# Products of zeros on TensorE in the first attention and the convolution of a four-layer kernel

## The reference

```python
x = x + L0_xattn(layernorm(x), ctx)     # first attention, convolution, MLP
x = x + L0_ffn(layernorm(x))            # 8 experts, 2 a token
x = x + L1_xattn(layernorm(x), ctx)     # second attention
x = x + L1_ffn(layernorm(x))            # 8 gated experts with low-rank parts
```

```python
scores = einsum(Q, K) / sqrt(32)                   # 4 heads, 64 x 64 a sequence
probs  = softmax(top 32 of 64 scores), scattered back
c      = mean over heads of probs @ (ctx @ Wv)
x      = layernorm(x) * (1 + g*scale_in) + g*shift_in   # scale, shift from c @ W_film
y      = causal convolution of x with K, per channel    # K from a sum of 64 exponentials
y      = y * (1 + g*scale_out) + g*shift_out            # from c @ W_film too
```

## Time and profile before

| | us |
|---|---|
| three executions | 932.19, 935.39, 935.05 |
| median | 935.05 |
| span of the profiled execution | 935.4 |
| mean granted clock in it | 0.799 |
| PE busy | 710.3 |
| DVE busy | 673.2 |
| POOL busy | 564.8 |
| ACT busy | 473.4 |

### The profile page before, as it was taken

One profiled execution on the slowest core, in us unless ns is written; L12 is line 12 of the kernel. 1 busy time (PEld: TensorE's weight loads), 2 busy tenths in 40 slices (PEclk: granted clock), 3 DMA queues, 4 the chain that ended last, 5 costly groups with the idle time before them and its releaser, 6 DMA issues. The chain is left out here.

```text
span 935.4 us, 20537 instructions
## 1 busy us (share of the span) xinstructions
PE 710.3 (76%) x6072; PEld 508.4 (54%) x6072; DVE 673.2 (72%) x3212; ACT 473.4 (51%) x1318; POOL 564.8 (60%) x931
## 2 busy tenths in 40 slices
PE   0686898979883999972498528998888874799970
PEld 0353554545483656631275426766666652699970
DVE  6898989978524688769111167598998887699974
ACT  3566576735200455450133175577777761577740
POOL 7688877766526544210677667345777767277770
PEclk9767787957555999996599855798988885899995
DMA  6300112997213977700365330000000002698928
GB/s 143 57 25 10 41 45 64 86 88 96 40 45 140 290 250 257 243 23 0 39 115 132 88 137 1 2 4 13 25 26 25 25 28 76 216 279 264 260 69 270
DMA packets 98829, 94.41 MB, mean 101 GB/s; under 512 B 37511, under 2 KB 82302, under 8 KB 98142
## 3 DMA queue, kind: packets, MB, share of 16 engines
q1 hardware_dynamic: 91268, 79.34, 33.1%
q0 software_dynamic: 6592, 13.58, 6.0%
q10 hardware_dynamic: 858, 0.17, 0.1%
HBM read 47.76 MB, written 43.19 MB: 97 GB/s over the span
## 5 line engine op out<-in xcount | busy, mean ns | idle before, releaser
L2402 POOL DMA_INDIRECT expert_pairs<-e_ys,e_home x78 | 75.4, 967 | 38.4 <-issue 23.5
L1742 POOL TENSOR_SCALAR a_kb<-a_kr,a_m,a_bk 128x128 f32<-128x128 f32 x128 | 57.9, 452 | 44.4 <-ACT a_kr L1981 32.3
L1760 POOL DMA_INDIRECT expert_slots<-r_rows,r_slotu x64 | 63.3, 989 | 30.3 <-DVE r_rows L2136 15.1
L950 DVE MATCH_REPLACE8 work<-m,work 128x64 f32<-128x64 f32 x384 | 75.7, 207 | 0.0
L1484 POOL DMA_INDIRECT ex_rows<-rows,slot_source x32 | 30.7, 960 | 52.7 <-POOLq L1163 43.2
L937 DVE MAX8 m<-work 128x8 f32<-128x64 f32 x384 | 57.0, 209 | 0.0
L825 PE MATMUL psf<-filmw,us 97*128 97x512 f32 x64 | 51.6, 902 | 3.0 <-ACT FO L846 2.9
L1815 PE MATMUL a_pss<-a_kb,a_qt 32*64 32x256 f32 x512 | 41.5, 463 | 13.9 <-ACT a_pp L1966 11.7
L2168 DVE TENSOR_REDUCE a_mx<-a_pss 128x8 f32<-128x512 f32 x64 | 43.9, 686 | 8.1 <-PE a_pss L1815 7.8
L2369 PE MATMUL e_ps<-e_XH,e_wh 128*128 128x256 f32 x156 | 48.1, 308 | 1.5 <-DVE e_XL L2414 1.5
L1536 ACT ACTIVATE ex_hs<-ex_psh,vec 128x512 f32<-128x512 f32 x32 | 22.0, 687 | 51.2 <-PE ex_psh L1517 50.5
(11 more groups left out here) (464 smaller groups left out, 2418.2 us busy)
## 6 DMA issues: line engine op xcount, KB each, us to landing
expert_slots<-rt_unfilled SPq DMA_DIRECT2D x151, 130.0 KB, 2.6
ahead<-folded_weights SPq DMA_DIRECT2D x20, 386.0 KB
e_wf<-folded_weights SPq DMA_DIRECT2D x19, 386.0 KB, 4.2
planes<-rt_zeros SPq DMA_DIRECT2D x4, 1024.0 KB
ew<-in_L_ffn_ew SPq DMA_DIRECT2D x16, 256.0 KB, 4.0
pair_y<-expert_pairs SPq DMA_DIRECT2D x16, 256.0 KB, 5.6
e_xr<-expert_slots SPq DMA_DIRECT2D x27, 130.0 KB, 3.3
folded_weights<-fold_done SPq DMA_DIRECT2D x8, 384.0 KB, 4.3
```

The source lines that it names most:

```text
L950: return own.did(dve.match_replace(wk_[x.j][:, h, :], m8[x.j][:, h, r, :], src[:, h, :], TAKEN))
L1742: m = pool.tensor_scalar(kb[a.j][:, :, h, :], k, m4[:, h:h + 1], bk4[:, h:h + 1], ALU.mult, ALU.add)
L1760: pool.indirect_dma_start(G.slots, bass.IndirectOffsetOnAxis(ap=slot[:, b, k, t:t + 1], axis=0), rb[b % NB][:, k, t, :], None).then_inc(se ...
L2402: pool.indirect_dma_start(G.pair, bass.IndirectOffsetOnAxis(ap=home[i % NY][:, k:k + 1], axis=0), ys[i % NY][:, k, :], None).then_inc(kept ...
```

## The change

A tile `still` of zeros, 128 x 256 in the type F32R (fp32 taken in one pass), is set once by POOL in setup. A helper `fill` issues n products of it, 128 x 128 by 256 columns, into a PSUM region; nobody reads the result. It is called: ahead of the scores (2 products), of the film product (2, and 8 for the last four tiles) and of the turn of `at` (2, and 8 for the last four), each time behind the wait for the bank and ahead of the wait for the data, which are exchanged for this; 12 products at the end of PE's program of the first attention; and 2 behind each of the 8 groups of the convolution, into a bank of their own.

```diff
+def fill(pe, G, out, n):
+    for _ in range(n):
+        pe.matmul(out, G.still[:, 0:P], G.still[:], start=True, stop=True)
...
                 pool.memset(G.dskip[:], 0.0).then_inc(s["memory"], 1)
+                pool.memset(G.still[:].bitcast(F32), 0.0)
                 pool.memset(K.zero, 0.0).then_inc(s["memory"], 1)
...
                     if score.real():
                         j = score.j
+                        after(pe, s["scores_kept"], score.t - 1)
+                        fill(pe, G, pss[j][:, 0:256], 2)
                         pe.wait_ge(s["qk_sb"], score.t + 1)
-                        after(pe, s["scores_kept"], score.t - 1)
...
                     if film.real():
                         j = film.j
+                        after(pe, s["film_sb"], film.t)
+                        fill(pe, G, psf[:, 0:256], 2 if film.t < NT - 4 else 8)
                         pe.wait_ge(s["u_sb"], film.t + 1)
-                        after(pe, s["film_sb"], film.t)
...
                     if attn.real():
+                        after(pe, s["u_sb"], attn.t - 1)
+                        fill(pe, G, psb[attn.j][:, 0:256], 2 if attn.t < NT - 4 else 8)
                         pe.wait_ge(s["attn"], attn.t + 1)
-                        after(pe, s["u_sb"], attn.t - 1)
...
                 march(slot, -3, NT + 3)
+                fill(pe, G, psa[0][:, 0:256], 12)
...
+        unread = C.ps("conv_unread", [P, 256], ctx)[:]
...
                     mm.then_inc(s["y"], 1)
+                    fill(pe, G, unread, 2)
...
+        G.still = C.sb("still", [P, 2 * P], F32R)
```

## The result

| | before | after |
|---|---|---|
| median of 20 runs each, us | 938.28 (929.89 to 944.89) | 932.21 (919.26 to 940.43) |
| ratio after/before | | 0.986, interval 0.983 to 0.989 |
| profiled execution: time, span, us | 935.39, 935.4 | 925.46, 924.2 |
| mean granted clock of the span | 0.80 | 0.85 |
| granted clock from 60 to 240 us | 0.75 | 0.91 |

The account below looks back on a forecast made before the run. DVE was taken to bound the attention at full clock and PE at half, PE the convolution. Attention -7.5, tail -0.5, convolution +1 and memset 0 summed to -7.0 us: 935.05 to 928.0 us, range 912 to 945.

Parts of the forecast that it names:

- Attention, -7.5 forecast: First attention: fills bring the clock back sooner, shortening DVE's stops on `ee`; -7.5 us, from a span of 1.5 to 10.6.
- Nothing below its 6.25 us a tile is to be had: First attention: DVE's busy time, at most 6.25 us for each of 32 tiles, taken as the limit on any gain.
- 3 x 2.8 + 3.3 + 1.7 + 0.3: PE's three attention slots with side pieces at full clock without fills: 13.7 us, against 18.8 us that DVE needs.
- the rival that forecast a loss: Attention slots stay at half clock around "first" and fills only cost; 944 us taken, 954 at worst; chance 0.18.
- "first": Side piece in every third attention slot, four pairs of products, 3.3 or 5.8 us; clock falls inside it were to stay.
- the one near 38: DVE stop of 2.2 us while the attention loop starts up, not PE's; forecast unchanged.
- the one near 195: DVE stop of 3.6 us, where ScalarE waits 5.5 us for a store of folded weights; forecast unchanged.
- The tail, -0.5 forecast: Last four attention tiles: three film products faster at full clock, less their fills; -0.5 us, between -3 and +3.
- the case at half clock: Twelve fills at the attention's end take 2.9 us at half clock, of which 1.1 us would show; 0 was taken.
- The convolution, +1 forecast: Convolution: one or two groups under 2.2 us, then 3.9 us each; +1 us in the sum.
- I let it fall: Convolution with two fills a group: the full clock handed over was taken to fall, after 3.5 us.
- The rival with a chance of 0.12: Clock holds throughout the convolution, all 8 groups at 1.94 us: -11.7 there, -11 in the attention, about 912 us; chance 0.12.

Follow-up runs that it names:

- the corner kernel: The changed kernel with every fill on 32 rows and 32 columns of zeros in place of 128 and 128; ratio 1.070 to the kernel before.
- the kernel with fills only at the end: The changed kernel without fills in the attention's tiles, keeping the 12 at its end and 2 behind each convolution group; ratio 0.993 to the kernel before.
- the pieces: The changed kernel with POOL's 128x1024 product cut into eight, plus 24 fills ahead of each of the first MLP's first two turns; ratio 0.982 to before.

## Why the prediction was right or wrong

**The frame held.** The kernel is faster, by the ratio more than the sum had it. DVE bounds the attention at full clock, PE bounds the convolution, and both depend on the clock. The waits for `ee` were forecast at 13 us and are 12.4 and 12.5 in two profiles, but 24.4 in the third; the clock between 60 and 240 us was forecast at 0.85 and is 0.91, 0.92 and 0.86. The exchanged waits and the memset cost nothing, as forecast, and the kernel with only these shows it.

**Attention, -7.5 forecast, -3.8 measured: mis-sized.** The stops shrank by 8.6 us, which is the mechanism and nearly the size. What was missing is the warning that the prediction itself gave at its end, a stop that moves without touching a term: 3.8 us came back as a longer `pr`, begun while POOL's products ran. "Nothing below its 6.25 us a tile is to be had" held DVE's own work for fixed, and it wasn't. The other profiles add that the gain there is some 3 us in the mean and scatters by more than that.

**The price of the fills: the product right, the change of kind mis-sized.** Behind its like a fill costs 0.12 us at full clock and 0.21 at half, as the row taken for it has it (0.12 and 0.24 forecast). But a fill stands among products of another kind: fp32 products of two records each, or other tile sizes. For that the prediction had 0.1 us a group in the convolution, with a bound of 0.2, and nothing in the attention; in the convolution it is 0.32 at full clock and 0.45 at half, by the groups with no, one and two fills. A pair thus costs 0.56 and 0.87 us a group. In the attention at full clock:
```profile
121.48 0.50 PE L192 MATMUL psb<-still 128*128 128x256 f32 x2
121.82 0.27 PE L849 MATMUL psb<-ident,at 128*128 128x128 f32 x1
121.85 0.48 PE L192 MATMUL pss<-still 128*128 128x256 f32 x2
122.26 0.65 PE L816 MATMUL pss<-kb,qt 128*64 128x256 f32 x4
```
0.34 and 0.41 us a pair, 0.24 of it the two products. Six a tile are thus 1.0 to 1.2 us and not 0.7, with three changes of kind a slot. It did no harm, since DVE bounds there at full clock (3 x 2.8 + 3.3 + 1.7 + 0.3 with 3 x 1.2 makes 17.3, still under 18.8); at half clock it would have made the rival that forecast a loss worse, and the corner kernel is that rival carried out: +7%.

**Which stops go.** Those around "first" behave as the prediction had it: between 90 and 130 us the waits go from 2.6 to 0.5 us (0.7 of the 2.4 near 118 had been forecast to stay). Of the two that were to stay, the one near 38 does, with 2.0 us in place of 2.2; the one near 195, behind the store of folded weights, shrinks from 3.6 to 2.2. Between 50 and 90 us nothing goes (4.4 us, before 4.3), and one stop there has grown from 2.3 to 3.2. The clock of 0.91 is more than the 0.85 that was to be left by the falls inside the side pieces; how many of these went wasn't counted.

**The tail, -0.5 forecast, -0.7 measured,** and the twelve at nothing: right, and for the reason given, since they end at 254.3, before POOL's last product ends at 254.7. The 1.1 us for the case at half clock came out as 0.5 in the kernel with fills only at the end (its convolution starts 1.0 us behind POOL, 0.5 is usual). The convolution was to start 8 us earlier and starts 4.5 us earlier, for want of the attention's share.

**The convolution, +1 forecast, -8.5 measured: the step that failed.** Two steps in it were right. The clock is handed over at full; and handed over without fills behind the groups it falls within 3.4 us (3.5 had been forecast with them). The failed one is "I let it fall" with two fills a group. It was argued from "first", where half of the records are full-size and the clock falls within some 3 us all the same. That comparison was of counts of records; it didn't ask what the other half was, products of 16 rows, nor what the fill's columns are, 256 of them; which of the two makes the difference no run tells. The runs put in its place that with two fills a group the clock stays at 1.00 to the end in every profile of the changed kernel, that with one it falls in the second group, and that with two at half clock it doesn't rise. The rival with a chance of 0.12 had this right, and its price of 1.94 us a group was too low by 0.48: 0.32 for the change of kind, and the 64 products at 1.86 us rather than 1.7. With -11.7 replaced by what was measured, -8.5, its 912 us would have been 915.

The Trainium skill, "TensorE: Matmul & The Clock Gate", Part 1, tells that sustained activity releases the clock. The traces here agree only if activity is not read as busy time alone: the corner fills had PE busy for 176.9 us of 180 at 0.59, the 64-by-64 products 27 us of 27 at 0.50.

**The sum.** -3.8 - 0.7 - 8.5 + 1.9 = -11.1, against -11.2 of span. That the forecast of -7.0 came as near as it did is luck, two errors of opposite sign: 3.7 us too much in the attention, 9.5 too little in the convolution. The +1.9 in the MLP had no term. It goes with the clock of the MLP's first eight wide products, which came back later (5.77 us for them, 4.83 before), a stage that the prediction took as it was.

**What stays open.** Which alignment of the engines decides between an attention of 204 and one of 212 us was not found; the same kernel shows both. Whether the convolution held its clock in the executions above 934 us was not seen. That `pr` is held up by POOL's products is shown by the timelines and by the pieces; what a kernel with the pieces alone would bring was not run. Why the twelve at half clock raised the clock once and not the other time is open as well.

## What to carry to other kernels

Filler products on TensorE are worth trying where a stage is bound by this engine at half clock, but with the full array, in a number that holds the clock to the end, and with a bridge over the idle stretch before the stage: each of these left out turned the gain in the convolution into a loss. Price a filler with the change of kind on both sides of it, beside its price in a row of its own kind. Judge such a change by whole executions as well as by the stage: the 8.5 us of the stage are in every profile, and the bare medians over 32 executions show a gain of 0.6 to 1.1%. And when a faster producer takes a consumer's stops away, look at what the consumer's instructions now run beside.

## What the runs showed of the hardware that was not expected

- 64-by-64 products, 512 back to back, ran 27 us at clock 0.50 and never raised it, and let a full clock fall within 3.4 us; two full-array products of 256 columns after every 64 of them held it for 19 us in every profile where it was full at the start, one did not.
- After 2.35 us of idleness the first group of 64 products (2.06 us) still ran at full clock, and the second at half (one execution).
- Products on a 32-by-32 corner take nearly the time of full ones at half clock (0.70 us a pair against 0.87) and left the clock at 0.59, where it was 0.75 without them and 0.91 with full ones.
- Fills of zeros and of ones came with the same clock (0.91 and 0.92).
- A one-record product of 256 columns costs 0.12 us behind its like at full clock and 0.21 at half; the change to it from 64-by-64 products and back costs 0.32 and 0.45 us more.
- VectorE's product of two operands in SBUF, 0.42 us by itself, took 2.01 us when it began 0.17 us behind a 1.90 us product on GpSimd, and 0.51 us where that one was cut in eight. When it began first, GpSimd's next product took 0.70 us in place of 0.45.
- Eight products of 512 columns at the start of the MLP took 3.4 to 5.8 us from one profile to the next, by when the full clock came back.
